# Graph network layer, edge loop: blocks padded to tiles of 128 edges instead of units of 256

## The reference

```python
hi = h[ei]                      # ei = src, ej = dst
hj = h[ej]
x = jnp.concatenate((hi, hj, d2), axis=-1)
msg = jax.nn.silu(x @ mW1 + mb1)
msg = _layer_norm(msg, ln_g, ln_b)
msg = jax.nn.silu(msg @ mW2 + mb2)
agg = jax.ops.segment_sum(msg, ei, num_segments=h.shape[0])
```

## Time and profile before

| | before |
|---|---|
| median of three runs | 1673.52 us (1671.7 to 1680.5) |
| span of the profiled execution | 1439.5 us |
| PE busy | 1279.5 us (89%) |
| DVE busy | 1182.8 us (82%) |
| ACT busy | 932.1 us (65%) |
| POOL busy | 878.1 us (61%) |
| edge loop, first L1061 to last L1723 | 337.8 to 1072.7 us |
| gathered rows, L752, 448 times | 444.2 us |

### The profile page before, as it was taken

How to read it: one execution, slowest core, us unless ns; L and a number is a source line. 1 busy time by engine, 2 the same in 40 slices (tenths; PEclk the granted TensorE clock), 3 DMA queues, 4 the chain that set the end, 5 groups by cost and what they waited for, 6 DMA issues and landing times.

```text
span 1439.5 us, 32698 instructions
## 1 busy us (share of the span) xinstructions
PE 1279.5 (89%) x8927; PEld 1149.6 (80%) x8928; DVE 1182.8 (82%) x3550; ACT 932.1 (65%) x1856; POOL 878.1 (61%) x885
## 2 busy tenths in 40 slices
PE   2678899996999999999999999999998847999990
PEld 1366778786999999999999999999886635988890
DVE  6999778726999999999999999999954688666662
ACT  0877444414778887888878888888753544666660
POOL 2188774035887778787777787878710014767761
PEclk7599999997999999999999999999999978999995
DMA  3911100022333333333333333336860162444447
GB/s 118 197 34 43 31 13 23 1 68 64 111 104 98 104 106 101 101 99 112 99 101 102 107 103 101 100 108 93 86 193 0 43 253 72 75 73 73 73 60 280
DMA packets 71387, 133.94 MB, mean 93 GB/s; under 512 B 23126, under 2 KB 43868, under 8 KB 70695
## 3 DMA queue, kind: packets, MB, share of 16 engines
q0 software_dynamic: 36560, 77.33, 24.1%
q1 hardware_dynamic: 33986, 52.62, 12.0%
q10 hardware_dynamic: 780, 3.24, 0.6%
HBM read 107.71 MB, written 25.29 MB: 92 GB/s over the span
## 4 chain that ended last, share of the span: by engine, by line
PE 71%; DVE 17%; DMA 4%; issue 3%; ACT 2%; POOL 1%; DVEq 0%; ACTq 0%; POOLq 0%; SPq 0%
PE ps L1071 12%; PE ps L832 9%; PE ps L1045 7%; PE ps L1049 7%; PE ps L1044 7%; PE ps L1061 7%; DVE place_val_t L1579 3%; DVE lane_hot_e_t L1574 2%; PE ps L1170 2%; PE ps L1201 2%; PE ps L1199 2%; PE ps L1200 2%; PE ps L1172 2%; PE ps L1171 2%; PE ps L1102 2%
## 5 line engine op out<-in xcount | busy, mean ns | idle before, releaser
L752 POOL DMA_INDIRECT msg_t<-dst_table,stage_idx x448 | 444.2, 991 | 128.7 <-issue 126.5
L1044 PE MATMUL ps<-w_hi_t,msg1T_hi_t 128*128 128x256 f32 x896 | 252.4, 303 | 0.0
L1338 ACT ACTIVATE msg1n_t<-msg_t,nw_b,nw_y 128x256 f32<-128x256 f32 x448 | 242.4, 590 | 0.0
L1350 ACT ACTIVATE msg_t<-msg_t 128x512 f32<-128x512 f32 x224 | 141.6, 632 | 149.4 <-DVE msg_t L1743 148.8
L1045 PE MATMUL ps<-w_lo_t,msg1T_hi_t 128*128 128x256 f32 x896 | 234.2, 283 | 0.0
L1071 PE MATMUL ps<-msg_t,hot_t 128*125 128x256 f32 x896 | 230.4, 379 | 0.2 <-issue 0.2
L1049 PE MATMUL ps<-w_hi_t,msg1T_lo_t 128*128 128x256 f32 x896 | 179.8, 282 | 0.0
L1045 PEld LDWEIGHTS ps<-w_lo_t,msg1T_hi_t 128*128 128x128 f32 x896 | 171.9, 192 | 0.0
L1044 PEld LDWEIGHTS ps<-w_hi_t,msg1T_hi_t 128*128 128x128 f32 x896 | 170.3, 190 | 0.0
L1738 DVE BATCH_NORM_STATS2 est<-msg_t 128x6 f32<-128x256 f32 x448 | 166.2, 413 | 1.2 <-ACT msg_t L1350 1.2
L1071 PEld LDWEIGHTS ps<-msg_t,hot_t 128*125 128x125 f32 x896 | 152.0, 187 | 14.2 <-issue 0.4
(11 more groups left out here) (374 smaller groups left out, 3081.1 us busy)
## 6 DMA issues: line engine op xcount, KB each, us to landing
near_rows<-row_list SPq DMA_DIRECT2D x44, 320.0 KB
w_sb_t<-in_L_ffn_W_dram SPq DMA_DIRECT2D x16, 512.0 KB, 8.5
msg_t<-dst_table,stage_idx POOLq DMA_INDIRECT x448, 2.8
res_t<-in_x_dram SPq DMA_DIRECT2D x1, 3125.0 KB
total<-zero_chunks_t SPq DMA_DIRECT2D x1, 3125.0 KB, 26.8
dst_table<-dst_stage SPq DMA_DIRECT2D x25, 125.0 KB
xm_table<-xm_t POOLq DMA_DIRECT2D x5, 625.0 KB, 7.5
sum_a_t<-total SPq DMA_DIRECT2D x5, 625.0 KB, 10.6
```

Source lines behind the costliest of these rows:

```text
L752: pool.indirect_dma_start(out=msg1[:, k, j, :], out_offset=None, in_=dst_table, in_offset=bass.IndirectOffsetOnAxis(stage_idx[:, G * k + j ...
L1044: pe.matmul(o[j], part(msg1T_hi, j, c), w2_hi[:, c, :], start=(c == 0), stop=False)
L1338: m = A(msg1n[:, (kl + 1) % 2, j, :], msg1[:, kk, j, :], ACT.Identity, bias=nw_b[:, kk, j:j + 1], scale=nw_y[:, kk, j:j + 1])
L1350: A(v, v, ACT.Silu).then_inc(msg1_sb, 1)
```

## The change

The lists of the blocks are padded to tiles of 128 edges. There are `TILES` = 424 tiles, still taken in pairs, so 212 units; the two tiles of a unit can belong to two blocks. Each tile has its own block number: `tile_blk` in place of `unit_blk`, five packed words a turn in place of three, and loads on PE before each second step. The sums of the two tiles are two results, and DVE adds them to `agg` one by one, the second behind the `msg1T_lo` step.

The statistics of both tiles are taken by one `bn_stats` that reads them alternately (`p j n -> p n j`), so that its even half is tile 0 and its odd half tile 1; `bn_aggr` is left out. POOL adds 256 times epsilon to the sums of squares before the power, so that the root is 1/16 of what it was; w2 is multiplied by 16, and the constant of the shift, now 1/16, is added by ACT in the copy and by DVE in `msg1T_lo`. The preparation works with tiles instead of units. Some tiles of SBUF are moved to other places.

```diff
-    UNITS = ((E + NB * GROUPS * (CHUNK - 1)) // CHUNK + NB * (UNIT_CHUNKS - 1)) // UNIT_CHUNKS
-    TILES = UNITS * G
+    TILE_CHUNKS = 128 // CHUNK
+    TILES = ((E + NB * GROUPS * (CHUNK - 1)) // CHUNK + NB * (TILE_CHUNKS - 1)) // TILE_CHUNKS
+    UNITS = TILES // G
...
             def roots(m, k, free):
-                pool.wait_ge(spread_ok, m // 2 + 1 if isinstance(m, int) else pairs + k // 2 + 1)
+                pool.wait_ge(spread_ok, m + 2)
...
+                st.did(pool.tensor_tensor(nw_v[:], est[:, k:k + 2, :, 2], eps_sum[:].rearrange("p (a b) -> p a b", b=G), ALU.add))
+                st.join()
                 pool.tensor_tensor(nw_y[:, k:k + 2, :], nw_v[:], minus_half[:].rearrange("p (a b) -> p a b", b=G),
                                    ALU.pow).then_inc(pow_ok, 1)
...
-                if k in (0, 4, 7):
-                    load_blocks(mybir.EngineType.PE, blk, n, k, 4 if k == 0 else 3)
+                if k % 2 == 0:
+                    load_blocks(mybir.EngineType.PE, blk, n, k, 2)
...
-                                          table[0:HR, bass.ts(blk[k], 1), :].rearrange("p a n -> p (a n)"),
+                                          table[0:HR, bass.ts(blk[k, j], 1), :].rearrange("p a n -> p (a n)"),
...
-                    after(pe, sum_sb, m_ - 1)
+                    after(pe, sum_sb, m_ * G - G)
                     for j in range(G):
-                        m = pe.matmul(bank(7 * (kl % 2), D, rows=NP), hot[:, kl % 2, j, 0:NP], msg2[:, kl % 2, j, :],
-                                      start=(j == 0), stop=(j == G - 1))
+                        m = pe.matmul(bank(7 * (kl % 2), D, rows=NP, first=j * D), hot[:, kl % 2, j, 0:NP], msg2[:, kl % 2, j, :],
+                                      start=True, stop=True)
...
-                    A(msg1T_hi[:, kl % 2], bank(3 + kl % 2), ACT.Copy).then_inc(msg1T_sb, 1)
+                    A(msg1T_hi[:, kl % 2], bank(3 + kl % 2), ACT.Copy, bias=1.0 / ROOT_D).then_inc(msg1T_sb, 1)
...
-                if k % 2 and here(n - 3, UNITS):
-                    slot = (k - 3) % TURN
-                    st.join()
-                    dve.tensor_scalar(nw_v[:], emv[:, slot:slot + 2, :, 1], EPS, None, ALU.add).then_inc(spread_ok, 1)
...
+                def add_sums(j):
+                    after(dve, sum_sb, (n - 9) * G + j)
+                    a = agg[0:NP, bass.ts(blk[k, j], 1), :].rearrange("p a n -> p (a n)")
+                    dve.tensor_tensor(a, a, bank(7 * ((k + 1) % 2), D, rows=NP, first=j * D), ALU.add).then_inc(sum_sb, 1)
+
                 if here(m_, UNITS):
                     dve.wait_ge(sum_ps, m_ + 1)
-                    after(dve, sum_sb, m_)
-                    a = agg[0:NP, bass.ts(blk[k], 1), :].rearrange("p a n -> p (a n)")
-                    dve.tensor_tensor(a, a, bank(7 * ((k + 1) % 2), D, rows=NP), ALU.add).then_inc(sum_sb, 1)
-                if pair_on:
-                    nw.join()
-                    dve.tensor_scalar(shifts, shifts, 1.0, None, ALU.add).then_inc(rstd_ok, 1)
+                    add_sums(0)
...
-                    dve.tensor_tensor(msg1T_lo[:, k % 2], bank(3 + k % 2), msg1T_hi[:, k % 2].bitcast(F32), ALU.subtract)\
-                       .then_inc(msg1T_lo_sb, 1)
+                    dve.scalar_tensor_tensor(msg1T_lo[:, k % 2], bank(3 + k % 2), 1.0 / ROOT_D, msg1T_hi[:, k % 2].bitcast(F32),
+                                             ALU.add, ALU.subtract).then_inc(msg1T_lo_sb, 1)
+                if here(n - 9, UNITS):
+                    add_sums(1)
...
-                    for j in range(G):
-                        st.did(dve.bn_stats(est[:, kk, j, :], msg1[:, kk, j, :]))
+                    dve.bn_stats(est_pairs[:, kk, :], msg1[:, kk].rearrange("p j n -> p n j")).then_inc(spread_ok, 1)
...
-                    for j in range(G):
-                        st.did(dve.bn_aggr(emv[:, kk, j, :], est[:, kk, j, :]))
```

More of the change, by code:

```diff
@@ L132, in gps_layer @@
         region("weights", 32 * 1024)
[L133 removed]
+        region("small", 10208)
         ctx.enter_context(nc.sbuf_tensor("arena", [128, (cursor[0] - base) // 4], F32))
@@ L845, in _ @@
             pe.wait_ge(prep_ok, UNITS_N_OK)
-            pe.matmul(bank(6, 1, rows=NB + 1, first=EC), earlier[0:NB, 0:NB + 1], unit_n[0:NB, :],
+            pe.matmul(bank(6, 1, rows=NB + 1, first=EC), earlier[0:NB, 0:NB + 1], tile_n[0:NB, :],
                       start=True, stop=True).then_inc(prep_ps, 1)
@@ L864, in _ @@
                     pe.wait_ge(prep_ok, UNITS_LE_OK)
-                    pe.matmul(bank(6, UNITS, rows=1), ones[0:NB, 0:1], unit_le[0:NB, :], start=True, stop=True)\
+                    pe.matmul(bank(6, TILES, rows=1), ones[0:NB, 0:1], tile_le[0:NB, :], start=True, stop=True)\
                       .then_inc(prep_ps, 1)
@@ L1510, in _ @@
             dve.wait_ge(prep_ps, FIRST_PS)
-            units = bank(6, 1, rows=NB + 1, first=EC)
-            dve.scalar_tensor_tensor(group_d[C], units.broadcast_to([NB + 1, GROUPS]), float(UNIT_CHUNKS), group_c[C],
+            tiles = bank(6, 1, rows=NB + 1, first=EC)
+            dve.scalar_tensor_tensor(group_d[C], tiles.broadcast_to([NB + 1, GROUPS]), float(TILE_CHUNKS), group_c[C],
                                      ALU.mult, ALU.add).then_inc(prep_ok, 1)
-            step(dve.tensor_tensor(unit_e[B], units[B], unit_n[B], ALU.add))
-            dve.tensor_scalar(unit_le[B], iota[B, 0:UNITS], unit_e[B], None, ALU.is_ge).then_inc(prep_ok, 1)
+            step(dve.tensor_tensor(tile_end[B], tiles[B], tile_n[B], ALU.add))
+            dve.tensor_scalar(tile_le[B], run_of[B, 0:TILES], tile_end[B], None, ALU.is_ge).then_inc(prep_ok, 1)
             dve.wait_ge(edges_in, 32)
@@ L1544, in _ @@
                     dve.wait_ge(prep_ps, UNITS_PS)
-                    step(dve.tensor_scalar(unit_blk[:], bank(6, UNITS, rows=1), float(NB - 1), None, ALU.min))
+                    step(dve.tensor_scalar(tile_blk[:], bank(6, TILES, rows=1), float(NB - 1), None, ALU.min))
                     dve.memset(nw_t[:], 1.0).then_inc(prep_ok, 1)
```

117 lines of the change are left out of this document (55 added, 62 removed).

## The result

The changed kernel takes 1563.05 us (median of 5 runs, 1560.6 to 1572.8), the kernel before, timed beside it, 1671.7 (1665.5 to 1680.5): a ratio of 0.9354, 95% interval [0.9324, 0.9385]. It is 6.5% faster, where 1696 us and "slower" were forecast.

A forecast was written before the change was run, and what follows sets the result against it. The prediction took DVE to bound the changed edge loop: 21.2 turns of 35.0 us make 742.0 us against 719.5 now, 22.5 us more on 1673.5, so 1696 us, with a range of 1642 to 1714.

The forecast's parts named there:

- The 234.0 us around the span: Median 1673.5 us minus profiled span 1439.5, taken to lie around the span and stay as it is.
- The sign of the forecast: Whole kernel: slower, 1696 us against 1673.5; chance of slower by over 0.5% 0.49, faster 0.28.
- PE 3.21 us a unit, a turn 32.1, DVE within 1%, POOL within 2%: Edge loop before: a turn is 10 units; all three engines nearly bound it, DVE's own work 31.9 us, POOL's 31.6.
- The statistics, 0.93 us from start to start: DVE's bn_stats of 512 values: 0.59 side by side plus 0.34 for reading two tiles alternately.
- The reduction's 0.66 ns a value: Extra price of strided reading, from a reduction of 400 values in 200-byte steps, applied to DVE's statistics as 0.34 us.
- The lower end of DVE's turn, 33.0 + 0.7: DVE's turn with the alternating read at 0.18 us: 33.7 us with the stall, loop 714 us, 5 less than now.
- The second addition, paid in full by DVE: DVE's extra addition to the sums each step, behind msg1T_lo, costed at 0.33 us from start to start.
- The stall for the block numbers, 0.7 us a turn: DVE's sequencer loading packed block numbers once a turn, kept at 0.7 us, 1.4 as upper end.
- POOL, 0.20 + 0.24 a pair: Epsilon addition ahead of each power on POOL: 0.20 us plus 0.24 wait for its result, making POOL's turn 33.8 us.
- The slack of 0.5 us a turn: Idle time in POOL's turn before the change, its own work being 31.6 us of 32.16.
- rival one (POOL the bound): Alternating read costs little or nothing, POOL's turn of 33.8 us decides: 1671 us, 3 less than now; chance 0.36.
- Fewer units, 38.6 us if PE bounds: Edge loop with 12 of 224 units gone: PE alone needs 680.9 us; whole kernel then 1635 us, chance 0.12.

The follow-up runs named there:

- the short and the long profile of before: Same unchanged kernel before, profiled twice: span 1439.5 us in the profile the prediction read, 1699.1 us when profiled again beside the follow-up kernels.
- b0_before: Kernel before, unchanged, profiled again beside the follow-up kernels: one execution of 1700.8 us with a span of 1699.1.
- a0_after: Changed kernel, unchanged, profiled on the same chip as the kernel before: one execution of 1569.1 us with a span of 1567.4.
- the two halves of the statistics part: Kernel before with only nw_v's release moved ahead of the msg1 addition: 1612.0 us; or only DVE's lighter statistics, epsilon at its old DVE place: 1609.2.
- the statistics part: Kernel before with one alternating bn_stats, no aggregation, epsilon on POOL, still 224 units: 1575.4 us, ratio 0.9279; where before took 1441 to 1443, 1457.1, ratio 1.0108.
- short sets: Groups of kernels timed together on one chip in which the unchanged kernel before took 1443 and 1441 us.
- long sets: Groups of kernels timed together on one chip in which the unchanged kernel before took 1672 to 1695 us.

## Why the prediction was wrong

**The 234.0 us around the span: the step that failed.** "The profile has no row for that part and the change doesn't touch it" took a difference between two numbers for a place. 1.7 us lie around the span; of the 259.6 us between the short and the long profile of before 175.1 were in the loop and 86.2 in the stage ahead of it. The change gained in the loop: in one set it went from 889.0 us (b0_before) to 757.7 (a0_after), 131.3 of the 131.7 us between the two spans. The sign of the forecast was lost here.

**PE 3.21 us a unit, a turn 32.1, DVE within 1%, POOL within 2%.** Right for the execution read, and PE's 3.21 also for the kernel before without gathers. In the timed ones a unit took 3.97 us, with PE 83% busy and DVE 77%. What ended last was, as the waits, the events and the two halves of the statistics part together suggest, a cycle: late signal, addition to msg1, nw_v, POOL's power, four gathers that make the next signal late. The prediction did say that releasing the power earlier "helps this engine only if it waits". POOL waited 73.6 us in 300.

**The statistics, 0.93 us from start to start: mis-sized.** They cost 0.61 to 0.62 (803.26 to 803.88), duration 699 ns, where 680 was named as "if nothing". The reduction's 0.66 ns a value doesn't carry over to this operation. The Trainium skill's rule on cachelines (SBUF — State Buffer, "Door 1: The DMA port swizzle") would count a crossing at every value. By the two-instruction form of before, 413 ns for 256 values, the step to 512 values cost 286 ns, about what 256 more values cost in the additions (0.26), so the trace doesn't bear the rule out for this read. A turn of DVE was therefore 3.1 us too long in the sum. (The lower end of DVE's turn, 33.0 + 0.7, has the 0.7 us for missing overlap in it as well; its own terms give 32.35 + 0.7.)

**The second addition, paid in full by DVE.** Right as DVE's time, 0.33 from start to start. In the short sets the changed kernel is 0.14 us a unit above the one without it.

**The stall for the block numbers, 0.7 us a turn.** Gone: the additions of the changed kernel in the short set have 0.5 us of idle time in 300 us (nearly nine turns) ahead of them. Where the load went wasn't tried; DVE waits for ACT in each step anyway.

**POOL, 0.20 + 0.24 a pair.** The addition takes 0.20 (right); the wait for its own result 0.08, a third of what the conversion had shown. The slack of 0.5 us a turn was right: 1.4 us more made the turn 0.85 us longer (32.97 against 32.12).

**What the sum had left out.** The chain DVE, ACT, DVE. With the statistics at 0.61, the prediction's own step of DVE is 2.465 + 0.61 = 3.08 us, below PE's 3.21; with POOL's addition at 0.28 its turn of POOL is 31.6 + 5 x 0.28 = 33.0. By its own terms rival one (POOL the bound) should have come true in the short sets. Without the second addition it did: 32.97 and 32.98 a turn. In the changed kernel it didn't: 34.27, since L1731 waits for ACT in every step. The loop went from 713.9 to 716.8 us, where the prediction had 719.5 to 742.0. There the direction was right (0.5% slower) and the size, 22.5 us, was too large by two errors of opposite sign.

**Fewer units, 38.6 us if PE bounds.** In the long sets they bring 48 us to the kernel before (12 x 4.0). In the changed kernel they and the second addition together move little: 1575.4 us with the statistics part to 1569.1 with everything (one execution).

## What to carry to other kernels

A gap between the span of a profile and the median of the runs is not a constant: before it is added to a forecast, the same kernel has to be profiled in the conditions in which it is timed. Where two engines hand work to each other each step, walk the ring once from start to start: an operation is free only if it lies outside the ring. A release that others wait for belongs ahead of an instruction that may itself have to wait. Where a term of the sum is corrected, the rivals are to be worked out again with it: here POOL's turn, and not PE's, was the next bound.

## What the hardware did that I had not expected

- While POOL issues indirect gathers, PE's semaphore increments came up to 3.7 us behind the modelled end of the matmul, several at once, in the loop of the long sets; in short sets, in loops without gathers and in the stages of a long execution without indirect transfers within 0.02 us. Powers of the same length on POOL did not do it. DVE's and ACT's increments in the same trace were in time.
- The kernel before takes 1672 to 1695 us or 1441 to 1443 us, by the set. The stage ahead of the loop differs too, by 86.2 us between the two profiles, and PE's signals are late in it as well while POOL issues indirect transfers. What decides between the two kinds is open; each of the five later sets was on another chip.
- Statistics over 512 values read alternately from two tiles 1024 bytes apart cost 699 ns; two over 256 values side by side 413 each.
